# Gate h of a graph network's pair of chunks: the reset state's part inside the seven products, and x's first rows loaded later

## The reference

```
for _ in range(5):
    a_in  = A   @ (state @ in_W.T  + in_b)
    a_out = A.T @ (state @ out_W.T + out_b)
    a = concat([a_in, a_out, state])
    r = sigmoid(a @ r_W.T + r_b)
    z = sigmoid(a @ z_W.T + z_b)
    joined = concat([a_in, a_out, r * state])
    h_hat  = tanh(joined @ h_W.T + h_b)
    state  = (1 - z) * state + z * h_hat
out = tanh(state @ o1_W.T + o1_b) @ o2_W.T + o2_b
result = layernorm(x + out)
```

## Time and profile before

| what | value |
|---|---|
| median of three runs | 996.21 us |
| profiled execution | 996.05 us, span 994.3 us |
| PE busy | 968.4 us (97%), 4480 matmuls |
| DVE busy | 738.5 us (74%) |
| ACT busy | 454.3 us (46%) |
| POOL busy | 36.8 us (4%) |
| granted PE clock, mean | 0.993 of 2.4 GHz |

### The profile page before, as it was taken

How to read it: one execution, slowest core, us unless ns; L and a number is a source line. 1 busy time by engine, 2 the same in 40 slices (tenths; PEclk the granted TensorE clock), 3 DMA queues, 4 the chain that set the end, 5 groups by cost and what they waited for, 6 DMA issues and landing times.

```text
span 994.3 us, 11827 instructions
## 1 busy us (share of the span) xinstructions
PE 968.4 (97%) x4480; PEld 442.0 (44%) x4480; DVE 738.5 (74%) x1156; ACT 454.3 (46%) x638; POOL 36.8 (4%) x43
## 2 busy tenths in 40 slices
PE   6999999999999999999999999999999999999995
PEld 3444444444444444444444444444444444445443
DVE  4999979888886587766758776776686687645756
ACT  3756656554345345523534553463345335412443
POOL 0310100000000000000000000000000010001100
PEclk9999999999999999999999999999999999999997
DMA  9998993234720454184025608601570681042101
GB/s 334 397 414 340 409 323 100 58 87 106 194 82 1 116 158 97 30 214 127 1 84 150 138 12 188 165 8 43 149 175 5 148 227 44 1 127 64 44 1 43
DMA packets 199112, 134.34 MB, mean 135 GB/s; under 512 B 61712, under 2 KB 191376, under 8 KB 194960
## 3 DMA queue, kind: packets, MB, share of 16 engines
q1 hardware_dynamic: 196752, 125.20, 43.3%
q0 software_dynamic: 2304, 8.39, 2.2%
HBM read 102.11 MB, written 16.78 MB: 120 GB/s over the span
## 4 chain that ended last, share of the span: by engine, by line
PE 90%; DVE 4%; ACT 2%; issue 2%; DMA 1%; SPq 1%; ACTq 0%; DVEq 0%
PE bank L1695 36%; PE bank L1824 19%; PE bank L1803 12%; PE bank L1637 11%; PE bank L1816 6%; PE bank L1835 4%; PE bank L1914 1%; DMA tmp<-in_adj 1%; PE bank L1895 1%; ACT areg L705 1%; SPq L375 0%; DVE pq_words L1058 0%; DVE tmp L953 0%; DVE areg L1216 0%; ACT sop_words L568 0%
## 5 line engine op out<-in xcount | busy, mean ns | idle before, releaser
L1695 PE MATMUL bank<-areg,xop_words 128*128 128x512 fp8e4 x1792 | 389.4, 379 | 2.9 <-DVE pq_words L1289 1.7
L1695 PEld LDWEIGHTS bank<-areg,xop_words 128*128 128x128 f16 x1792 | 174.8, 98 | 215.1 <-issue 2.6
L705 ACT ACTIVATE areg<-pq_words 128x512 f16<-128x512 f32 x90 | 56.3, 629 | 176.8 <-DVE pq_words L1289 73.6
L1824 PE MATMUL bank<-areg,pq_words 128*128 128x512 f16 x504 | 119.2, 379 | 0.7 <-DVE areg L1325 0.7
L1637 PE MATMUL bank<-areg,xop_words 128*128 128x512 fp8e4 x512 | 112.9, 383 | 4.2 <-ACT areg L539 4.2
L1824 PE MATMUL bank<-areg,w 128*128 128x512 f16 x378 | 90.9, 379 | 0.5 <-DVE areg L1325 0.5
L1325 DVE SCALAR_TENSOR_TENSOR areg<-pq_words,areg 128x512 f16<-128x512 f32 x90 | 63.1, 702 | 32.3 <-ACT areg L705 30.6
L1637 PEld LDWEIGHTS bank<-areg,xop_words 128*128 128x128 f16 x512 | 50.3, 99 | 66.2 <-issue 7.7
L539 ACT ACTIVATE areg<-tmp 128x2048 fp8e4<-128x2048 int32 x32 | 61.1, 1910 | 36.4 <-DMA tmp<-in_adj 18.7
L1824 PEld LDWEIGHTS bank<-areg,pq_words 128*128 128x128 f16 x504 | 49.2, 98 | 60.4 <-DVE areg L1325 1.2
L1803 PE MATMUL bank<-pq_words,w 128*128 128x512 f16 x288 | 65.4, 379 | 0.0
(11 more groups left out here) (207 smaller groups left out, 1206.7 us busy)
## 6 DMA issues: line engine op xcount, KB each, us to landing
areg<-kept_operands SPq DMA_DIRECT2D x112, 512.0 KB, 4.3
tmp<-in_adj SPq DMA_DIRECT2D x16, 1024.0 KB, 7.1
tmp<-in_adj_t SPq DMA_DIRECT2D x16, 1024.0 KB, 7.8
kept_operands<-xop_words POOLq DMA_DIRECT2D x11, 512.0 KB, 7.9
areg<-in_x SPq DMA_DIRECT2D x8, 512.0 KB, 6.8
kept_operands<-areg SPq DMA_DIRECT2D x4, 1024.0 KB, 10.3
kept_operands<-tmp POOLq DMA_DIRECT2D x5, 512.0 KB, 3.3
pq_words<-in_gate_w SPq DMA_DIRECT2D x6, 384.0 KB, 6.0
```

The source lines that it names most:

```text
L705: nc.scalar.activation(y_dst(t, g, name)[:, 0, :], src, ACT.Copy, scale=PSC).then_inc(s_yh, 1)
L1695: last = nc.tensor.matmul(dst[:, :], xop[:, m // 2, operand_block(xo, part, m % 2), :], place8[:, mo, m, :], start=first and m == pairs[0] ...
L1824: last = nc.tensor.matmul(dst[:, :], weights(d, wp), yop[:, d, Y_PLACE[name], xp, :], start=False, stop=final and d == 1 and (wp, xp) == P ...
```

## The change

It does two things.

1. r times state enters gate h in the paired form. DVE forms the sums t1 to t4 of the reset state (`pair_reset_sum`), ACT and DVE split seven operands into halves in six pieces (`RS_ORDER`; t1 and t2 together), and each of gate h's seven products carries 3 matmuls with them at its end. `pair_state` is gone. ACT's order in the gates is new: after the first sigmoid only y11's hi half is made, the others come behind the fourth sigmoid and the copy. On DVE the lo halves stand between the degree parts of gate h, and the kept parts between gate h's sums. The places that hold the halves are partly in the ends of `areg`.
2. Since x's rows are loaded into the same ends of `areg`, `load_rest(0)` and `load_rest(1)` move from the start of step 4 to the place ahead of the operands for its group 3, behind a wait for pair 0's last gate tile.

```diff
+RS_ORDER = ("y11", "y22", "t12", "t3", "y21", "t4")
...
-        rs_pair = tmp[:, 4 * CW:8 * CW].bitcast(F16).rearrange("p (c s f n) -> p c s f n", c=2, s=2, f=FT)
+        rs_block = tmp[:, 4 * CW:8 * CW].bitcast(F16).rearrange("p (o s n) -> p o s n", o=4, s=2)
+        rs_t12 = areg[:, half + tg_words:].bitcast(F16).rearrange("p (o s n) -> p o s n", o=2, s=2)
+        rs_t3 = areg[:, tg_words + CW:half].bitcast(F16).rearrange("p (s n) -> p s n", s=2)
...
                 if t == LAST:
                     sp.wait_ge(s_xl, 2 * CH * LAST)
                     sp.dma_start(b2_all, o2_b.partition_broadcast(P)).then_inc(s_b2, 16)
-                    load_rest(0)
-                    load_rest(1)
                 for at in range(4 * (t - 1) + 1, 4 * t + 1):
+                    if at == 4 * LAST - 1:
+                        sp.wait_ge(s_gate, GT * (CH * LAST + 2))
+                        load_rest(0)
+                        load_rest(1)
                     if at < 4 * LAST:
                         load_group(at)
...
             def pair_gates(t, p):          # ACT
...
-                for i in range(3):
+                pair_act(t, p, 0, 0)
+                pair_reset_hi(t, p, "y11")
+                for i in range(1, 4):
                     pair_act(t, p, 0, i)
-                    pair_reset_hi(t, p, i)
-                pair_act(t, p, 0, 3)
                 pair_copy(t, p, 1)
-                pair_reset_hi(t, p, 3)
+                pair_reset_hi(t, p, "y22")
+                pair_reset_hi(t, p, "t12")
+                pair_reset_hi(t, p, "t3")
+                pair_reset_hi(t, p, "y21")
                 pair_seed(t, p, 2, 0)
+                pair_reset_hi(t, p, "t4")
...
+            def pair_reset_sum(t, p, name):          # DVE
+                n, first = pair_at(t, p), 4 * pair_index(t, p)
+                b11, b12, b22, b21 = [r_pair[:, i, :] for i in range(4)]
+                if name == "t1":
+                    dve.wait_ge(s_rs, FT * n + 2)
+                    nc.vector.tensor_tensor(sum_1, b12, b11, ALU.subtract).then_inc(s_rt, 1)
+                elif name == "t3":
+                    dve.wait_ge(s_rs, FT * n + 3)
+                    nc.vector.tensor_tensor(sum_v, b22, b12, ALU.subtract).then_inc(s_rt, 1)
+                elif name == "t2":
+                    dve.wait_ge(s_rt, first + 1)
+                    nc.vector.tensor_tensor(sum_u, b22, sum_1, ALU.subtract).then_inc(s_rt, 1)
+                else:
+                    dve.wait_ge(s_rs, FT * n + 4)
+                    dve.wait_ge(s_rt, first + 3)
+                    nc.vector.tensor_tensor(b12, b21, sum_u, ALU.subtract).then_inc(s_rt, 1)
...
             def pair_product(t, p, gate, dst, name, weights, final=False):          # PE
...
+                if gate == 2:
+                    half_name = "t12" if name in ("t1", "t2") else name
+                    pe.wait_ge(s_rsl, rs_before(pair_at(t, p)) + RS_ORDER.index(half_name) + 1)
+                    for wp, xp in PASSES:
+                        last = nc.tensor.matmul(dst[:, :], weights(2, wp), rs_at[name][:, xp, :], start=False,
+                                                stop=final and (wp, xp) == PASSES[-1], skip_group_check=True)
                 return last
-            def pair_state(t, p, s):
-                f, c = PAIR_TILES[s]
-                pe.wait_ge(s_rsl, FT * pair_at(t, p) + 4)
-                for k in range(FT):
-                    for wp, xp in PASSES:
-                        last = nc.tensor.matmul(pair_banks[2][s][:, :], w16[:, 2 * FT + k, wp, feat(2 * FT + f)],
-                                                rs_pair[:, c, xp, k, :], start=False,
-                                                stop=k == FT - 1 and (wp, xp) == PASSES[-1], skip_group_check=True)
-                last.then_inc(s_gate, 1)
```

More of the change, by code:

```diff
@@ L150, in gnn_program @@
         r_pair = tmp[:, 0:4 * CW].rearrange("p (i n) -> p i n", i=4)
-        rs_pair = tmp[:, 4 * CW:8 * CW].bitcast(F16).rearrange("p (c s f n) -> p c s f n", c=2, s=2, f=FT)
+        rs_block = tmp[:, 4 * CW:8 * CW].bitcast(F16).rearrange("p (o s n) -> p o s n", o=4, s=2)
+        rs_t12 = areg[:, half + tg_words:].bitcast(F16).rearrange("p (o s n) -> p o s n", o=2, s=2)
+        rs_t3 = areg[:, tg_words + CW:half].bitcast(F16).rearrange("p (s n) -> p s n", s=2)
+        rs_at = {"y11": rs_block[:, 0], "y22": rs_block[:, 1], "y21": rs_block[:, 2], "t4": rs_block[:, 3],
+                 "t1": rs_t12[:, 0], "t2": rs_t12[:, 1], "t3": rs_t3}
         w_full = tmp[:, 0:2 * GD].rearrange("p (k m) -> p k m", k=FT)
@@ L274, in pair_index, with rs_before @@
             return 2 * (t - 1) + p
+        def rs_before(n):
+            t, c = n // CH, n % CH
+            if t == 0:
+                return FT * n
+            pairs = 2 * (t - 1) + (1 if c >= 2 else 0)
+            return FT * CH + len(RS_ORDER) * pairs + (FT * (c - 2) if t == LAST and c > 2 else 0)
         def state_done(n, f):
@@ L767, in pair_act @@
                 act.wait_ge(s_gate, GT * n + 4 * gate + i + 1)
-                if gate < 2 and s == 2:
+                if s == 2:
                     act.wait_ge(s_g22, pair_unit(t, p, gate) + 1)
@@ L773, in pair_act, with pair_reset_hi @@
                                      bias=bias_sb[:, 4 + gi:5 + gi], scale=UG).then_inc(s_act, 1)
-            def pair_reset_hi(t, p, i):
-                s = PAIR_ORDER[0][i]
-                f, c = PAIR_TILES[s]
-                act.wait_ge(s_rs, FT * pair_at(t, p) + i + 1)
-                nc.scalar.activation(rs_pair[:, c, 0, f, :], r_pair[:, s, :], ACT.Identity, scale=SIGX) \
-                    .then_inc(s_rsh, 1)
+            def pair_reset_hi(t, p, name):
+                n, sums = pair_at(t, p), 4 * pair_index(t, p)
+                if name in ("y11", "y22", "y21"):
+                    tile = {"y11": 0, "y22": 2, "y21": 3}[name]
+                    act.wait_ge(s_rs, FT * n + tile + 1)
+                    src, dst = r_pair[:, tile, :], rs_at[name][:, 0, :]
+                elif name == "t12":
+                    act.wait_ge(s_rt, sums + 3)
+                    src, dst = rs_sums_12, rs_t12[:, :, 0, :]
+                elif name == "t3":
+                    act.wait_ge(s_rt, sums + 2)
+                    src, dst = sum_v, rs_t3[:, 0, :]
+                else:
+                    act.wait_ge(s_rt, sums + 4)
+                    src, dst = r_pair[:, 1, :], rs_at["t4"][:, 0, :]
+                nc.scalar.activation(dst, src, ACT.Identity, scale=SIGX).then_inc(s_rsh, 1)
             def pair_gates(t, p):
@@ L1541, in pair_gates @@
                     pair_degree(t, p, 1, s)
-                for i in range(3):
-                    pair_reset(t, p, i)
-                    pair_reset_lo(t, p, i)
+                pair_reset(t, p, 0)
+                pair_reset_lo(t, p, "y11")
+                pair_reset(t, p, 1)
+                pair_reset_sum(t, p, "t1")
+                pair_reset(t, p, 2)
+                pair_reset_sum(t, p, "t3")
+                pair_reset_sum(t, p, "t2")
                 pair_reset(t, p, 3)
                 pair_sum_u(t, p, 1)
-                pair_reset_lo(t, p, 3)
                 pair_sum_12(t, p, 1)
+                pair_reset_lo(t, p, "y22")
+                pair_reset_sum(t, p, "t4")
+                pair_sum_22(t, p, 1)
+                pair_reset_lo(t, p, "t12")
                 pair_degree(t, p, 2, 0)
-                pair_sum_22(t, p, 1)
-                for s in range(1, 4):
-                    pair_degree(t, p, 2, s)
-                for i in range(4):
-                    pair_keep(t, p, i)
+                pair_reset_lo(t, p, "t3")
+                pair_degree(t, p, 2, 1)
+                pair_reset_lo(t, p, "y21")
+                pair_degree(t, p, 2, 2)
+                pair_reset_lo(t, p, "t4")
+                pair_degree(t, p, 2, 3)
+                pair_keep(t, p, 0)
                 pair_sum_u(t, p, 2)
+                pair_keep(t, p, 1)
                 pair_sum_12(t, p, 2)
+                pair_keep(t, p, 2)
                 pair_sum_22(t, p, 2)
+                pair_keep(t, p, 3)
                 pair_update(t, p, 0)
@@ L1824, in pair_product @@
                         last = nc.tensor.matmul(dst[:, :], weights(d, wp), yop[:, d, Y_PLACE[name], xp, :],
[L1825 removed]
+                                                start=False,
+                                                stop=final and gate < 2 and d == 1 and (wp, xp) == PASSES[-1],
                                                 skip_group_check=True)
[L1827 to L1838 removed]
+                if gate == 2:
[4 more added lines that the diff above has]
+                                                stop=final and (wp, xp) == PASSES[-1], skip_group_check=True)
+                return last
             def pair_gate(t, p, gate):
```

45 lines of the change are left out of this document (17 added, 28 removed).

## The result

| | before | changed |
|---|---|---|
| median | 996.13 us (6 runs, 995.06 to 997.0) | 1000.15 us (6 runs, 997.7 to 1001.57) |
| ratio, 95% interval | | 1.0038 [1.0028, 1.0048] |
| profiled execution, span | 996.05, 994.3 us | 997.70, 995.9 us |
| PE, DVE, ACT busy | 968.4, 738.5, 454.3 us | 963.4, 767.1, 465.4 us |

The changed kernel is slower by 0.38%, 4.0 us. The forecast was 998.2 us in a range up to 1001.7. The profiled execution is the fastest of its six runs, 2.45 us under the median, so its trace has to be read with that in mind.

The account below looks back on a forecast made before the run. PE, busy 97% of the span, was taken as the bound. The terms -4 x 0.647 + 3 x 1.59 - 0.2 = +1.98 us gave 998.0 for the profiled execution, 998.2 us against the median; range 995.0 to 1001.7.

Parts of the forecast that it names:

- Matmuls removed: Gate h falls from 66 to 63 matmuls per pair, 0.647 us less each; kept behind pair 0 in steps 1 to 4.
- DVE's and ACT's added work costs nothing: Ahead of gate h: 4.8 us more on DVE per pair, hidden by gate z with 2.4 us smallest margin; cost 0.
- The order inside gate h: Pair 1: tile 1 done after 45 matmuls instead of 36, 1.94 us later; 0.35 regained, so DVE's tail 1.59 us late.
- the main rival: After pair 1: late transposes do not hold PE longer, so pair 1 comes out even; 993.4 us, chance 0.12.
- The term 3 x 1.59: PE waits for the large transposes after pair 1 of steps 1 to 3: 1.59 us lost each, +4.77 us.
- x's term of -0.2: Start of step 4: moving x's two loads away from step 3's last transpose gives back 0.2 us; new place costs 0.
- The clock: Rival: PE's new 2.2 us gaps after pair 1 lower the granted clock, 1.7 us each, 1000 to 1003.4 us; chance 0.18.
- Half the delay: DVE's tail after pair 1 regains more, 0.9 us left per pair 1, within 0.1 us of before; chance 0.09.
- DVE as the bound: Rival: in gate z or h PE waits for DVE; one product waiting 1 us gives about 1004 us; chance 0.05.

Follow-up runs that it names:

- pair0_only: Changed kernel with the new gate h form in pair 0 alone, pair 1 in the old form, x's loads at the new place: 994.36 us, ratio 0.998 to before.
- tail_longer: Kernel before plus three useless DVE subtractions ahead of the large transposes' lo halves after pair 1 of steps 1 to 3: 1003.97 us, ratio 1.0077.
- late_tiles: Kernel before with y21's six matmuls moved ahead of the reset part of tiles 1 and 2 in pair 1's gate h: 997.98 us, ratio 1.0033.
- loads_only: Kernel before with only x's first two loads and their wait moved ahead of step 4's group 3 operands: 997.39 us, ratio 1.0009.
- pair1_only: Changed kernel with the new gate h form in pair 1 of steps 1 to 3 alone, pair 0 in the old form: 1003.41 us, ratio 1.0074 to before.
- filler: Changed kernel plus eight matmuls in PE's wait for the large transposes in steps 2 to 4, output wrong: 998.72 us, ratio 1.0027 to before.
- tail_filler: Kernel before plus three useless DVE subtractions in the tail after pair 1 and eight filling matmuls in PE's break, output wrong: 1001.73 us, ratio 1.0058.

## Why the prediction was right, and where it was short

**Matmuls removed:** 21, and 0.65 us per pair where nothing waits behind. Right, in four places of the table, and alone in pair0_only.

**DVE's and ACT's added work costs nothing:** right. DVE's busy time rose by 28.6 us, not 7 x 4.8 = 34: rows that stand back to back overlap (398.06 to 398.73 is a pitch of 0.67 us for rows of 0.75), and the sum of durations counts the overlap twice. The smallest margin is 2.35 us for the 2.4 forecast.

**The order inside gate h:** right in each link. The first tanh starts 9.92 us after gate h's start (forecast 9.9). From tile 1's z times h (409.91) to tile 0's (414.70) it is 4.79 us, and 1.33 from there to the next (416.03), so the 0.35 us were regained. The first large transpose was forecast for 421.96; 0.76 us earlier (0.11 start, 0.65 pair 0, which the forecast's times of step 1 left out) is 421.20, and 421.19 was measured. The last one then went out 12.1 us after PE left gate h (forecast 11.5); the 0.6 us are the first one's longer issue. The steps 2 and 3 lose 1.59 and 1.55 us (forecast 1.59). That this chain holds PE at all, which the main rival denied, tail_longer and late_tiles show by two other causes.

**Two terms were mis-sized.**
- The term 3 x 1.59: the first of the three, step 1's, cost 2.16. The 0.57 more are the first large transpose's issue, 3.66 us for 3.05; loads_only has the same without the new form. The prediction asked of the moved loads only what they do at their new place, where it put their cost at 0, and looked for nothing in step 1.
- x's term of -0.2 was -0.05. It was read from a difference of 0.2 us between three breaks, and the third break stays at 0.49 to 0.55 where the loads are gone.

With both the sum is -2.6 + 4.77 + 0.57 - 0.05 = +2.7, the loop's +2.70.

**The clock.** What is left to the medians' +4.0 and +3.5 is 0.8 to 1.3 us. The clock was a rival at 0.18, with 1.7 us a fall as its price; three falls seen in pair1_only and tail_longer cost 1.69 each, behind breaks of 2.84, 2.09 and 2.33 us. In both profiled executions of the changed kernel the clock stayed at 1.00 behind all three breaks, as this window of the first shows (columns as above):

```profile
434.00:438.00 4.00, 4.00 (x20) 1.84 (x19) 2.27 (x4) 0.63 (x1) 0.00 (x0) 1.00 0.94 265
```

These are the fastest and the third fastest of its eleven runs. The slower ones have a lower mean clock (the group at 0.993 or less lies 2.2 us above the other in the median), but the mean does not say where the clock was low. The kernel before has the same two groups: of its 24 runs on the first chip seven have 0.993 or less and lie at a median of 997.87, the others at 995.37, and its profiled execution, at 0.993 too, has no break over 0.54 us in the loop and a clock of 1.00 there. Its low stretches are near the start and at the head, and both places scatter in every kernel. PE reaches the break of 0.66 us, ahead of the first pair's gate h, at 286.1 to 286.4 us in seven of the twelve profiled executions and at 287.0 to 290.3 in five. The clock over 20 to 30 us was 0.83 or 1.00 in those seven and 0.66 to 0.69 in those five, as here in the kernel before and in tail_longer (start at 289.32):

```profile
20.00:30.00 10.00, 9.09 (x35) 3.85 (x36) 9.82 (x22) 8.06 (x12) 0.00 (x0) 0.83 1.00 394
...
20.00:30.00 10.00, 9.04 (x29) 3.50 (x30) 9.82 (x22) 8.12 (x12) 0.00 (x0) 0.66 1.00 396
```

The head's 24 matmuls took 2.79 to 5.30 us. For falls behind the breaks speaks how often the mean is low: in 7 of 11 runs of the changed kernel, in 11 of the 54 of before that ran beside the experiments, in 1 of 11 of filler. So the 0.8 to 1.3 us fit a rival that holds in a part of the executions, but no trace of the changed kernel shows a fall, and what they are made of is open. Here the Trainium skill ("TensorE: Matmul & The Clock Gate", on HAM oscillation) said that the gaps in which TensorE waits for data can put the array back to its slow clock. The trace of before did not show it behind its gap of 1.90 us at 137 us, those of pair1_only and tail_longer do, in three of six breaks.

The median of 1000.15 us lies outside the forecast's own 997.2 to 999.2 and inside the wider range that the clock's rival asked for. The terms that were right give +2.2, the first transpose adds 0.6, and the rest of the +4.0 is the open part. That the wider range held is in this part luck.

**Half the delay, and DVE as the bound:** neither. The delay is whole, and no product waits.

The version for pair 0 alone beats both kernels: 994.36 us with the new form in four pairs, 994.23 in three with x's loads in place. They are the same within their intervals, since the fourth pair's 0.65 us is lost to step 1's longer issue.

## What to carry to other kernels

Count not only the matmuls that a new form saves but, for every output tile, after which matmul it is finished: here 3 fewer matmuls per pair were worth 0.65 us, and 9 later for the first tile cost 1.6 us, because a chain over ACT, DVE, SP and the DMA starts at that tile and ends where PE waits. Use the shorter form where nothing waits behind it, and keep the old order where something does. A break of PE of about 2 us may cost more than its length: behind three of twelve here the clock fell, for 1.69 us each. Work put into such a break costs nothing as long as it ends within the wait. And before a lower mean clock is laid on the breaks, look at the same runs of the kernel before, and at the start and the end of the traces.

## What the runs showed of the hardware

- The profiled executions of pair1_only, tail_longer and the changed kernel (twice) have twelve breaks of 1.80 to 2.84 us. The clock fell behind three of them (2.84, 2.09, 2.33), for 1.69 us each. Behind the breaks of 0.3 to 1.5 us in filler, tail_filler, late_tiles and pair0_only it stayed at 1.00. The length alone does not decide: near the start, behind gaps of 3.65 and 3.68 us at 21 us, the clock over 20 to 30 us was 1.00 in the changed kernel and in pair0_only, and behind one of 3.65 us at the same place in tail_filler it was 0.66.
- The issue of the first large DMA transpose of step 1 takes 3.05 to 3.08 or 3.60 to 4.01 us on SP, and which of them goes with the place of two loads that are issued some 450 us later. In each long one a packet of the instruction queue falls into the issue, in no short one. The large transposes of steps 2 and 3 in the changed kernel took 3.00 and 3.04 us.
- POOL's adds of x's bias, now beside DVE's work, slow it. The changed kernel's timeline at 871:

```profile
871.64 7.78 POOL L540 TENSOR_TENSOR areg<-areg,diag_words 128x256 f32<-128x256 f32 x8 [637.42 <-DMA areg<-in_x]
...
877.74 1.09 DVE L1229 SCALAR_TENSOR_TENSOR pq_words<-pq_words 128x512 f16<-128x512 f32 x1
...
879.74 0.69 DVE L1229 SCALAR_TENSOR_TENSOR pq_words<-pq_words 128x512 f16<-128x512 f32 x1
```

The same instruction takes 1.09 us while POOL adds and 0.69 us when it has ended. In the kernel before, where POOL is idle there, both take 0.69 (at 875.14 and 876.20); loads_only has 1.09 and 0.69 again. PE did not wait for it.
